# Graph layer with gathers, one-hot picks and sorted scatter: the broadcast of dst is issued one step earlier and first in SyncE's step

## The chip, the cores and the metric

The kernel runs on one core of one Trainium2 chip, written directly against the five engines (TensorE, VectorE, ScalarE, GpSimd, SyncE) with hand-placed semaphores. The metric is the device time of one execution in microseconds (us), median of three runs.

## The reference

```python
h = jnp.maximum(_layernorm(x, axis=-1), 0.0)                 # x: 100000 x 96
concat = jnp.concatenate([h[src], h[dst], edge_attr], axis=-1)   # 25000 edges, 96 + 96 + 64
gates = jax.nn.sigmoid(concat @ W_e + b_e)                   # 25000 x 96
messages = jax.nn.softplus(concat @ W_n + b_n)
gated = gates * messages
h_new = jax.ops.segment_sum(gated, dst, num_segments=n)
edge_count = jnp.clip(segment_sum(ones, dst), 1.0, None)[:, None]
x = x + h + h_new / edge_count
```

All edges are sorted by `dst`.

## The kernel before, in words

The 100000 nodes are cut into 49 chunks of 2048 rows (`CHUNK`, 16 tiles of 128 rows by 96), and the 25000 edges into 49 steps (`STEPS`) of 512 edges (`TB` = 4 tiles of 128). Every engine runs its own `step(i)` loop over the same index, each a few steps ahead of or behind the others, and semaphores tie them together.

What each engine does in one step:

- **SyncE (SP)** issues all plain transfers of the step from one queue: the edge attributes (`attr`), the load of node chunk i (`node_x`, 768 KB), the store of finished node chunk i - 4 (`out<-node_out`, 768 KB), and two broadcasts. `low_across` is two stretches of 400 values of the low bits of `dst`, each copied to all 128 partitions (2 x 200 KB). `dst_across` is the 512 `dst` values of one edge step, copied to all partitions (256 KB). The only thing that paces SP is the wait for `node_sum_done`, ahead of the node load: the buffer of chunk i - 4 must be read out.
- **VectorE (DVE)** finishes the layer norm factors of a chunk, normalizes 3 of its 16 tiles, then does for edge step m = s - 3 (s is its own step): `same` (line 732, which compares `dst_across` with the `dst` column, and waits for that broadcast), `same_prev`, `messages` (the product of gate and softplus). Then 13 statistics of the next node chunk (line 703), `onehot` (line 762, from `low_across`, and waits for it), the sum `node_out` (line 801), which raises `node_sum_done`, then the edge statistics, the counts and `final` of edge step m, and the variance.
- **TensorE (PE)** picks the normalized rows of the destinations with the one-hot matrix (`picks`, line 950, 2 x 8 tiles), transposes the source rows and attributes, sums the messages of equal `dst` (`sums`, lines 962 and 963, which waits for `messages` and `same`), and computes the products `z` (lines 1016 to 1018).
- **ScalarE (ACT)** normalizes the other 13 tiles and does the exponentials and logarithms.
- **GpSimd (POOL)** gathers four tiles of source rows (line 396) and scatters four tiles of `final` with accumulation into `out` (line 417).

`dst_across` and `onehot` have two buffers each, `low_across` and `same` one, `node_x` and `node_out` four. Semaphore names used below: `same_done` counts two for each edge step that DVE has compared, `onehot_done` one for each one-hot matrix.

In step index: SP's step i is released by the node sum of DVE's step i - 5. DVE's step s compares edge step s - 3, and makes the one-hot matrix of chunk s + 2. The loop of DVE that uses what SP's step i brings:

```python
def equality(m):
    wait(dve, across_loaded[m % 2], m // 2 * 16 + 16)
    wait(dve, sum_done, m)
...
def one_hot(n):
    wait(dve, low_loaded, 32 * (n + 1))
    wait(dve, pick_done, 2 * (n - 1))
```

Of the kernel before, what the change touches and what calls it, by code (L numbers as in the profile page):

```python
# [10 lines left out]
P = 128  # L11
# [4 lines left out]
TB = 4  # L16
STEPS = TILES // TB
# [25 lines left out]
def build(nc, x, src, dst, edge_attr, w_e, b_e, w_n, b_n, out, count_table, dst_pad, low_pad):  # L43
    ctx = ExitStack()
    with ctx:
        def sb(name, shape, dt=FP32):
            return ctx.enter_context(nc.sbuf_tensor(name, shape, dt))
# [4 lines left out]
        def sem(name):  # L52
            return ctx.enter_context(nc.semaphore(name))

        def sems(name, n=NS):
            return [sem(f"{name}{u}") for u in range(n)]
# [58 lines left out]
        dst_across = [sb(f"dst_across{v}", [P, TB, P], I32) for v in range(2)]  # L115
# [61 lines left out]
        dst_stored = sem("dst_stored")  # L177
# [17 lines left out]
        across_loaded = sems("across_loaded", 2)  # L195
# [34 lines left out]
        same_done = sem("same_done")  # L230
# [37 lines left out]
        def runs_step(i):  # L268
            return 0 <= i < STEPS
# [10 lines left out]
        def wait(eng, semaphore, value):  # L280
            if value > 0:
                eng.wait_ge(semaphore, value)

        def chunk_dmas(n):

            return 16 * (n // NS + 1) + (16 if n == STEPS - 1 else 0)

        def move_chunk(eng, n, t, tile, inward, done):
            lo = n * CHUNK
            if n < STEPS - 1:  # L290
                parts = [(t[lo:lo + CHUNK, :].rearrange("(r p) d -> p r d", p=P), tile[:, :, :])]
            else:
                mid = lo + LAST_FULL * P
                parts = [(t[lo:mid, :].rearrange("(r p) d -> p r d", p=P), tile[:, 0:LAST_FULL, :]),
                         (t[mid:NODES, :], tile[0:LAST_PART, LAST_FULL, :])]
            for far, near in parts:
                eng.dma_start(near if inward else far, far if inward else near).then_inc(done, 16)  # L297

        def load_index_rows(eng, n, t, shift_by, loaded):
            half = P * P  # L300
            full = (TILES - 1) * P
            k = LAST_EDGES - shift_by
            eng.dma_start(index_rows[:, n, 0, :], t[shift_by:shift_by + half].rearrange("(t e) -> t e", e=P)).then_inc(loaded, 16)
            eng.wait_ge(padding_done, 1)
            eng.dma_start(index_rows[0:TILES - 1 - P, n, 1, :],
                          t[half + shift_by:full + shift_by].rearrange("(t e) -> t e", e=P)).then_inc(loaded, 16)
            eng.dma_start(index_rows[TILES - 1 - P:TILES - P, n, 1, 0:k],
                          t[full + shift_by:EDGES].rearrange("(a e) -> a e", a=1)).then_inc(loaded, 16)

        dst_flat = dst_pad.rearrange("t e -> (t e)")  # L310
        low_flat = low_pad.rearrange("t e -> (t e)")

        def first_at(eng, cell):
            return eng.value_load(cell, min_val=0, max_val=TILES * P)  # L314

        @block.sync
        def _(sp):
            load_index_rows(sp, 0, dst, 0, dst_rows_loaded)

            def load_low(n):  # L320
                first, second = (first_at(sp, first_row[0:1, 2 * n + h:2 * n + h + 1]) for h in range(2))
                wait(sp, onehot_done, n)
                for h, at in ((0, first), (1, second)):
                    sp.dma_start(low_across[:, h, :],  # L324
                                 low_flat[bass.ds(at, SPAN)].partition_broadcast(P)).then_inc(low_loaded, 16)

            def step(i):
                n = i - LEAD
                tail = (STEPS - 1) * TB * P
                if runs_step(n):  # L330
                    wait(sp, attr_trans_done, n - NS + 1)
                    if n == STEPS - 1:
                        m = (TB - 1) * P
                        sp.dma_start(attr[n % NS][:, 0:TB - 1, :],
                                     edge_attr[tail:tail + m, :].rearrange("(t p) f -> p t f", p=P)).then_inc(attr_loaded[n % NS], 16)
                        sp.dma_start(attr[n % NS][0:LAST_EDGES, TB - 1, :],
                                     edge_attr[tail + m:EDGES, :]).then_inc(attr_loaded[n % NS], 16)
                    else:
                        ev = edge_attr[0:tail, :].rearrange("(b t p) f -> b p t f", t=TB, p=P)
                        sp.dma_start(attr[n % NS][:, :, :], ev[n, :, :, :]).then_inc(attr_loaded[n % NS], 16)  # L340
                j = i - NS
                if runs_step(j):
                    wait(sp, node_sum_done, j + 1)
                if runs_step(i):
                    move_chunk(sp, i, x, node_x[i % NS], True, node_loaded[i % NS])
                if runs_step(j):
                    move_chunk(sp, j, out, node_out[j % NS], False, node_stored[j % NS])
                if i == 0:
                    load_index_rows(sp, 2, dst, 1, next_rows_loaded)
                if i == NS - 1:  # L350
                    sp.wait_ge(place_done, 2)
                    sp.dma_start(first_row[0:1, :].rearrange("a (p b) -> a p b", b=1),
                                 place_i[0:HALVES, BLOCKS:BLOCKS + 1]).then_inc(place_loaded, 16)
                    sp.dma_start(place_row[0:1, :].rearrange("a (p b) -> a p b", b=BLOCKS),
                                 place_i[0:HALVES, 0:BLOCKS]).then_inc(place_loaded, 16)
                    sp.wait_ge(place_loaded, 32)
                    sp.wait_ge(low_stored, 16)
                    load_low(0)
                n = i - 2
                if i >= NS - 1 and runs_step(n):  # L360
                    load_low(n)

                k = i - 7
                if runs_step(k):
                    if k == 0:
                        sp.wait_ge(dst_stored, 16)
                    wait(sp, same_done, 2 * (k - 1))
                    sp.dma_start(dst_across[k % 2][:, :, :].rearrange("p t e -> p (t e)"),
                                 dst_flat[k * TB * P:(k + 1) * TB * P].partition_broadcast(P)).then_inc(across_loaded[k % 2], 16)

            for i in range(STEPS + 7):
                step(i)
            for u in range(NS):
                sp.wait_ge(node_stored[u], chunk_dmas(STEPS - 1 - (STEPS - 1 - u) % NS))
# [704 lines left out]
```

## Time and profile before

| | |
|---|---|
| median of three runs | 948.62 us (947.77 to 948.77) |
| profiled execution, its own time | 951.04 us |
| span of the profiled execution | 949.3 us |
| mean granted TensorE clock | 0.792 |
| TensorE matmul busy | 605.9 us, 64% of the span |
| VectorE busy | 546.1 us, 58% |
| ScalarE busy | 520.5 us, 55% |
| GpSimd busy | 512.4 us, 54% |
| data moved | 136.32 MB, mean 144 GB/s |

The busy times are those of the profiled execution; shares are of its span. The loop's steps look alike from about 100 us to 870 us, so that one step read in detail stands for all.

### The profile page before, as it was taken

How to read it: one execution, taken by the hardware profiler on the slowest of the kernel's cores; microseconds unless marked ns; L12 is line 12 of the kernel's file. 1: busy time of each engine (PE TensorE's matmuls, PEld its weight loads, DVE VectorE, ACT ScalarE, POOL GpSimd, SP SyncE). 2: the span in 40 equal slices, each digit the busy share in tenths (PEclk: the TensorE clock that was granted, in tenths of full speed). 3: DMA queues.
4: the chain of work that ended last, by engine and by line, in shares of the span. 5: the costliest groups of instructions: out<-in, count | busy, mean ns of one | idle time of the engine just before them, and what ended most of it. 6: DMA issues, size and time to landing. Idle time of an engine off the chain costs nothing.

```text
span 949.3 us, 15042 instructions
## 1 busy us (share of the span) xinstructions
PE 605.9 (64%) x3832; PEld 578.3 (61%) x3832; DVE 546.1 (58%) x2203; ACT 520.5 (55%) x1330; POOL 512.4 (54%) x404
## 2 busy tenths in 40 slices
PE   0255777667656765775776677567667657758971
PEld 0255777567556765764766566567667656747871
DVE  5667466466546645654664665466466456548551
ACT  0356655655564565466456546645655654665660
POOL 5211355654565466466556546655654664666676
PEclk9997778878777787778787778778778777878795
DMA  8277757766785677687577668767866865875652
GB/s 202 55 176 162 156 126 166 161 138 141 159 158 125 151 165 149 132 176 154 124 165 164 137 136 173 152 122 160 164 143 148 165 150 125 182 150 121 113 82 18
DMA packets 285403, 136.32 MB, mean 144 GB/s; under 512 B 262207, under 2 KB 275848, under 8 KB 285320
## 3 DMA queue, kind: packets, MB, share of 16 engines
q1 hardware_dynamic: 249214, 116.34, 52.8%
q0 software_dynamic: 34576, 18.40, 14.4%
q10 hardware_dynamic: 1530, 0.61, 0.3%
q8 instruction: 35, 0.57, 0.3%
q14 instruction: 48, 0.39, 0.1%
HBM read 88.16 MB, written 48.30 MB: 144 GB/s over the span
## 4 chain that ended last, share of the span: by engine, by line
DMA 33%; SPq 26%; DVE 26%; issue 8%; PE 3%; POOL 2%; DVEq 0%; ACT 0%; POOLq 0%; ACTq 0%
DMA dst_across<-dst_pad 30%; SPq L324 11%; SPq L297 10%; DVE stats L703 9%; DVE node_out L801 9%; SPq L314 6%; DVE messages L725 3%; DVE onehot L762 3%; POOL out L417 2%; DMA low_across<-low_pad 2%; PE pick_ps L950 1%; DVE same_prev L735 1%; DVE dst_t L645 1%; DMA dst_t<-dst_pad,first_tile_i 1%; DMA dst_t<-in_src 1%
## 5 line engine op out<-in xcount | busy, mean ns | idle before, releaser
L417 POOL DMA_INDIRECT out<-final,scatter_idx x196 | 309.7, 1580 | 317.9 <-DVE final L717 251.1
L962 PE MATMUL sums_ps<-messages,same 128*128 128x97 f32 x392 | 123.3, 415 | 247.5 <-DVE messages L725 247.5
L484 ACT ACTIVATE node_out<-node_x,shift,rstd 128x96 f32<-128x96 f32 x637 | 261.7, 458 | 12.5 <-DVE shift L756 12.5
L396 POOL DMA_INDIRECT edge_x<-in_x,src_idx x196 | 200.6, 1023 | 111.2 <-issue 58.8
L962 PEld LDWEIGHTS sums_ps<-messages,same 128*128 128x128 f32 x392 | 99.7, 312 | 254.1 <-DVE messages L725 254.0
L732 DVE TENSOR_TENSOR same<-dst_across,dst_col 128x512 f32<-128x512 int32 x49 | 34.0, 693 | 327.6 <-DMA dst_across<-dst_pad 327.6
L950 PE MATMUL pick_ps<-onehot,node_out 128*96 x1568 | 165.2, 263 | 61.0 <-ACT node_out L484 44.9
L950 PEld LDWEIGHTS pick_ps<-onehot,node_out 128*96 128x96 f32 x1568 | 156.6, 178 | 77.5 <-issue 77.2
L490 ACT ACTIVATE log_var<-var 128x20 f32<-128x20 f32 x52 | 11.4, 218 | 321.1 <-DVE var L827 321.1
L703 DVE BATCH_NORM_STATS2 stats<-node_x 128x6 f32<-128x96 f32 x784 | 142.2, 243 | 0.0
L963 PE MATMUL sums_ps<-messages,same_prev 128*128 128x97 f32 x392 | 118.4, 402 | 0.0
L1016 PE MATMUL z_ps<-w_src,src_t 97*128 97x192 f32 x392 | 117.8, 388 | 0.0
L1017 PE MATMUL z_ps<-w_dst,dst_t 96*128 96x192 f32 x392 | 109.5, 365 | 0.0
L1018 PE MATMUL z_ps<-w_attr,attr_t 128*128 128x192 f32 x392 | 104.9, 351 | 0.0
L963 PEld LDWEIGHTS sums_ps<-messages,same_prev 128*128 128x128 f32 x392 | 101.8, 318 | 0.0
L801 DVE TENSOR_TENSOR node_out<-node_out,node_x 128x1536 f32<-128x1536 f32 x49 | 85.8, 1750 | 5.9 <-PE pick_ps L950 5.9
L1017 PEld LDWEIGHTS z_ps<-w_dst,dst_t 96*128 96x128 f32 x392 | 83.5, 225 | 0.0
L1016 PEld LDWEIGHTS z_ps<-w_src,src_t 97*128 97x128 f32 x392 | 83.1, 236 | 0.0
L1018 PEld LDWEIGHTS z_ps<-w_attr,attr_t 128*128 128x128 f32 x392 | 79.1, 214 | 0.0
L514 ACT ACTIVATE src_h<-edge_x,shift,rstd 128x96 f32<-128x96 f32 x196 | 74.9, 452 | 1.8 <-DVE shift L756 1.8
L502 ACT ACTIVATE dst_t<-pick_ps 96x336 f32 x98 | 43.4, 443 | 52.0 <-PE pick_ps L950 44.7
L549 ACT ACTIVATE log1p<-log1p 128x768 f32<-128x768 f32 x49 | 41.3, 842 | 0.1
(107 smaller groups left out, 624.1 us busy)
## 6 DMA issues: line engine op xcount, KB each, us to landing
node_x<-in_x SPq DMA_DIRECT2D x48, 768.0 KB, 5.2
out<-node_out SPq DMA_DIRECT2D x48, 768.0 KB, 7.8
low_across<-low_pad SPq DMA_DIRECT2D x98, 200.0 KB, 6.0
dst_across<-dst_pad SPq DMA_DIRECT2D x49, 256.0 KB, 6.2
attr<-in_edge_attr SPq DMA_DIRECT2D x48, 128.0 KB, 6.4
edge_x<-in_x,src_idx POOLq DMA_INDIRECT x196, 2.8
out<-final,scatter_idx POOLq DMA_INDIRECT x196, 6.1
node_x<-in_x SPq DMA_DIRECT2D x1, 624.0 KB
```

The lines of the kernel that those rows point to most:

```text
L324: sp.dma_start(low_across[:, h, :], low_flat[bass.ds(at, SPAN)].partition_broadcast(P)).then_inc(low_loaded, 16)
L396: nc.gpsimd.indirect_dma_start(out=edge_x[i % NS][:, t, :], out_offset=None, in_=x, in_offset=bass.IndirectOffsetOnAxis(ap=src_idx[:, i * ...
L417: nc.gpsimd.indirect_dma_start(out=out, in_=final[j % FINALS][:, t, :], in_offset=None, out_offset=bass.IndirectOffsetOnAxis(ap=scatter_id ...
L484: last = nc.scalar.activation(node_out[n % NS][:, r, :], node_x[n % NS][:, r, :], ACT.Relu, bias=shift[us][:, c:c + 1], scale=rstd[us][:, ...
L703: last = nc.vector.bn_stats(stats[:, TB + r, :], node_x[c % NS][:, r, :])
L801: nc.vector.tensor_tensor(node_out[d % NS][:, :, :], node_out[d % NS][:, :, :], node_x[d % NS][:, :, :], ALU.add).then_inc(node_sum_done, 1)
L950: last = nc.tensor.matmul(pick_ps[0:D, bass.ds(a, WINDOW)], node_out[d % NS][:, h * BLOCKS + b, :], onehot[d % 2][:, h, bass.ds(a, WINDOW) ...
L962: nc.tensor.matmul(sum_ps[:, t, :], same[:, t, :], cur, start=True, stop=False)
L963: last = nc.tensor.matmul(sum_ps[:, t, :], same_prev[:, t, :], prev, start=False, stop=True)
L1016: nc.tensor.matmul(z, src_t[0:D + 1, t, :], w_src[0:D + 1, :], start=True, stop=False)
L1017: nc.tensor.matmul(z, dst_t[0:D, e:e + P], w_dst[0:D, :], start=False, stop=False)
L1018: last = nc.tensor.matmul(z, attr_t[:, t // 2, :], w_attr[t % 2][:, :], start=False, stop=True)
```

## The change

SP's block for the broadcast of `dst` moves within the step, and its index changes from i - 7 to i - 6. It is issued after the wait for `node_sum_done` and ahead of the node load and store; the code of the broadcast itself is the same, and SP's loop is one step shorter. No other engine's code is touched.

```diff
                 if runs_step(j):
                     wait(sp, node_sum_done, j + 1)
+                k = i - 6
+                if runs_step(k):
+                    if k == 0:
+                        sp.wait_ge(dst_stored, 16)
+                    wait(sp, same_done, 2 * (k - 1))
+                    sp.dma_start(dst_across[k % 2][:, :, :].rearrange("p t e -> p (t e)"),
+                                 dst_flat[k * TB * P:(k + 1) * TB * P].partition_broadcast(P)).then_inc(across_loaded[k % 2], 16)
                 if runs_step(i):
                     move_chunk(sp, i, x, node_x[i % NS], True, node_loaded[i % NS])
                 if runs_step(j):
...
                 if i >= NS - 1 and runs_step(n):
                     load_low(n)

-                k = i - 7
-                if runs_step(k):
-                    if k == 0:
-                        sp.wait_ge(dst_stored, 16)
-                    wait(sp, same_done, 2 * (k - 1))
-                    sp.dma_start(dst_across[k % 2][:, :, :].rearrange("p t e -> p (t e)"),
-                                 dst_flat[k * TB * P:(k + 1) * TB * P].partition_broadcast(P)).then_inc(across_loaded[k % 2], 16)
-
-            for i in range(STEPS + 7):
+            for i in range(STEPS + 6):
                 step(i)
```

On SP, in the middle of the program, one step of the kernel before reads so (the attributes first, the broadcast of `dst` last):

```order
L340 DMA attr<-in_edge_attr 128x4x64 [waits attr_trans_done]
L297 DMA node_x<-in_x 128x16x96 [waits node_sum_done]
L297 DMA out<-node_out 128x16x96
L314 TENSOR_LOAD dst_t
L314 ISA x2
L324 REGISTER_ALU [waits onehot_done]
L324 DMA low_across<-low_pad 128x400
L324 REGISTER_ALU
L368 DMA dst_across<-dst_pad 128x512 [waits same_done]
```

The same step of the changed kernel:

```order
L340 DMA attr<-in_edge_attr 128x4x64 [waits attr_trans_done]
L349 DMA dst_across<-dst_pad 128x512 [waits same_done,node_sum_done]
L297 DMA node_x<-in_x 128x16x96
L297 DMA out<-node_out 128x16x96
L314 TENSOR_LOAD dst_t
L314 ISA x2
L324 REGISTER_ALU [waits onehot_done]
L324 DMA low_across<-low_pad 128x400
L324 REGISTER_ALU
```

(In both, the pair of register loads and the low broadcast stand twice; one of each is left out.) The broadcast has moved from behind both low broadcasts to the head of what the node sum releases, and it now carries both waits.

On DVE, which waits for both broadcasts, nothing moves. One step of it reads in both kernels, from the end of the normalization on:

```order
L787 TENSOR_SCALAR node_out<-node_out 128x288 [waits dve_part_done]
L732 TENSOR_TENSOR same<-dst_across,dst_col 128x512 [waits sum_done,across_loaded0]
L735 TENSOR_TENSOR same_prev<-dst_across,dst_col 32x4x32 [waits ones_done]
L725 TENSOR_TENSOR messages<-log1p 128x4x96 [waits sum_done,ones_done,softplus_done,gate_done]
L703 BN_STATS stats<-node_x 128x6 x13
L762 TENSOR_SCALAR onehot<-low_across,lane 128x800 [waits pick_done,low_loaded]
L801 TENSOR_TENSOR node_out<-node_out,node_x 128x1536 [waits pick_done,dve_norm_done,node_norm_done]
```

What moved is which of SP's steps fills the buffer that `same` reads: before, SP's step that is released by the node sum of the step just ahead of this one; after, the one before that.

## Rows read from the trace of the kernel before

**Rows 1.** The page: busy share of two engines, and the chain by engine.

```profile
PE 605.9 (64%) x3832; PEld 578.3 (61%) x3832; DVE 546.1 (58%) x2203; ACT 520.5 (55%) x1330; POOL 512.4 (54%) x404
...
DMA 33%; SPq 26%; DVE 26%; issue 8%; PE 3%; POOL 2%; DVEq 0%; ACT 0%; POOLq 0%; ACTq 0%
```

**Rows 2.** The waits of all engines: total us, times, longest.

```profile
DVE same L732 <- DMA dst_across<-dst_pad: 327.6, 46, 9.4
...
DVE onehot L762 <- DMA low_across<-low_pad: 17.0, 4, 5.2
```

**Rows 3.** The waits of SP's own queue.

```profile
SPq L297 <- DVE node_out L801: 533.0, 49, 12.9
```

**Rows 4.** Timeline of one step: start, busy us, engine, line, what, idle before.

```profile
399.14 1.75 DVE L801 TENSOR_TENSOR node_out<-node_out,node_x 128x1536 f32<-128x1536 f32 x1
...
400.92 0.38 SPq L297 DMA_DIRECT2D node_x<-in_x  x1
...
401.35 1.67 SPq L297 DMA_DIRECT2D out<-node_out  x1
...
403.60 1.62 POOL L417 DMA_INDIRECT out<-final,scatter_idx  x1 [5.83 <-DVE final L717]
...
404.67 2.22 SPq L324 DMA_DIRECT2D low_across<-low_pad  x2
...
405.50 0.36 DVE L787 TENSOR_SCALAR node_out<-node_out 128x288 f32<-128x288 f32 x1
...
406.93 0.43 SPq L368 DMA_DIRECT2D dst_across<-dst_pad  x1
...
407.40 1.57 PE L950 MATMUL pick_ps<-onehot,node_out 128*96 x16
...
413.58 0.69 DVE L732 TENSOR_TENSOR same<-dst_across,dst_col 128x512 f32<-128x512 int32 x1 [7.72 <-DMA dst_across<-dst_pad]
...
415.10 2.17 DVE L703 BATCH_NORM_STATS2 stats<-node_x 128x6 f32<-128x96 f32 x13
...
415.40 0.94 POOL L396 DMA_INDIRECT edge_x<-in_x,src_idx  x1 [0.30 <-issue]
...
417.18 0.62 DVE L762 TENSOR_SCALAR onehot<-low_across,lane 128x800 f32<-128x800 f32 x1
...
417.72 1.75 DVE L801 TENSOR_TENSOR node_out<-node_out,node_x 128x1536 f32<-128x1536 f32 x1
```

**Rows 5.** The chain that ended last, same step: issue of the second low broadcast.

```profile
406.53 0.35 SPq L324
```

**Rows 6.** Transfers issued between 400 and 418.6 us: size, median us to landing.

```profile
low_across<-low_pad SPq DMA_DIRECT2D x2, 200.0 KB, 6.4
dst_across<-dst_pad SPq DMA_DIRECT2D x1, 256.0 KB, 6.6
```

**Rows 7.** Timeline of DVE in an early step, ahead of the first dst broadcast.

```profile
59.41 1.75 DVE L801 TENSOR_TENSOR node_out<-node_out,node_x 128x1536 f32<-128x1536 f32 x1
...
71.86 0.64 DVE L762 TENSOR_SCALAR onehot<-low_across,lane 128x800 f32<-128x800 f32 x1 [3.56 <-DMA low_across<-low_pad]
```

**Rows 8.** Timeline of DVE: first and last node sum around 43 steps with a dst broadcast.

```profile
87.37 1.76 DVE L801 TENSOR_TENSOR node_out<-node_out,node_x 128x1536 f32<-128x1536 f32 x1 [1.72 <-PE pick_ps L950]
...
872.19 1.75 DVE L801 TENSOR_TENSOR node_out<-node_out,node_x 128x1536 f32<-128x1536 f32 x1
```

**Rows 9.** Timeline of POOL at the end of the program.

```profile
902.67 1.55 POOL L417 DMA_INDIRECT out<-final,scatter_idx  x1 [4.28 <-DVE final L717]
...
912.84 1.55 POOL L417 DMA_INDIRECT out<-final,scatter_idx  x1 [3.02 <-DVE final L717]
```

**Rows 10.** Windows: busy us of each engine, then PEclk, DMA share, GB/s.

```profile
411.70:413.60 1.90, 0.00 (x0) 0.00 (x0) 0.02 (x1) 1.90 (x5) 1.44 (x2) 0.50 1.10 241
...
100.00:870.00 770.00, 517.76 (x3296) 494.64 (x3295) 449.52 (x1812) 444.80 (x1143) 433.57 (x333) 0.78 0.70 150
```

## The prediction

> **What bounds the kernel now.** I read the page first: no engine is near full, TensorE is the busiest with 64% [rows 1], and the chain that ended last runs for a third through transfers and for a quarter each through SP's issuing and DVE. So it is a loop of latencies, not of work. The waits name the transfer: DVE waited 46 times for the broadcast of dst, 327.6 us in all, or 7.1 us a step; for the low broadcast only four times [rows 2]. SP in turn waited all 49 times for the node sum, 533.0 us [rows 3]. These two waits close the loop.
>
> The timeline of one step shows it whole [rows 4]. The node sum ends at 399.14 + 1.75 = 400.89 us. SP issues the node load at 400.92, the store at 401.35, the low broadcasts from 404.67, the second of them at 406.53 [rows 5], and at 406.93 the dst broadcast. DVE has been ready for it since 405.50 + 0.36 = 405.86, and starts `same` at 413.58, so the broadcast is taken to land there, 12.69 us behind the node sum. Then come `same`, messages and 13 statistics, `onehot` at 417.18, and the next node sum at 417.72. The step took 18.58 us; 43 such steps took 872.19 - 87.37 = 784.82 us, 18.25 each [rows 8].
>
> **What the change does to a step.** The broadcast that `same` needs was issued in the same DVE step that waits for it. Now it is issued one node sum earlier, so it has a whole step more and the 7.1 us wait goes. Its buffer is free: SP's step i now waits until edge step i - 8 has been compared, and DVE does that in its step i - 5 ahead of the very node sum that releases SP. So `same_done` should never be the later of the two waits, and costs nothing; if it were late, the node load, the store and both low broadcasts would stand behind it.
>
> The stall does not go whole, because `onehot` waits for the low broadcasts of the same SP step, which is released by the node sum just ahead. Today that wait is covered by the dst wait and the work behind it. What is late next is therefore the second low broadcast. DVE would have its statistics done 417.18 - 413.58 = 3.60 us after it starts `same` at 405.86, at about 409.5, and then stands until the low broadcast lands.
>
> When does it land? Today it was issued at 406.53, and the two of this window took 6.4 us in the median [rows 6]: 412.9. The moved issue costs SP 0.43 us ahead of it [rows 4], so by its issue it lands at 406.53 + 0.43 + 6.4 = 413.36. `onehot` then starts at 413.36 instead of 417.18: **3.82 us less a step**. I take this value. From below and above:
>
> - If the broadcast of dst holds up all that is behind it by its own transfer time, the last of the queue lands when the last of the queue landed before, at 413.58. The same bytes from the same release must be moved. Saving 3.60 us.
> - In the early step without a dst broadcast and with no scatter yet, `onehot` started at 71.86, 10.72 us behind the node sum's end at 59.41 + 1.75 [rows 7]. That was for 768 + 768 + 400 = 1936 KB; 256 KB more at this rate is 1.42 us, so 12.14 us, landing at 413.03. Saving 4.15 us. It leaves out the scatters, so I hold it for the optimistic end.
>
> The Trainium skill ("DMA: Bandwidth & Descriptors", section on queues, rings and completion order) says that each DMA engine consumes the descriptors of one ring in order. That speaks for the first of these, against my 3.82. By that rule the sum is some 9 us smaller; this trace agrees so far as the dst broadcast, issued last, lands 0.65 us behind the second low one. I stay between the two because the dst broadcast also no longer shares the engines with the end of the low ones.
>
> **Is there other cover for 3.8 us?** The step would be 18.25 - 3.82 = 14.43 us. POOL from its first scatter to its last gather needs 415.40 + 0.94 - 403.60 = 12.74 us [rows 4]; it fits with 1.7 us to spare. DVE's own work is 546.1 / 49 = 11.1 us, TensorE's 605.9 / 49 = 12.4 us [rows 1]. TensorE had its second picks done at 407.40 + 1.57 = 408.97, 8.1 us into the step, so they are not late for a node sum at 12 to 13 us. The node load has one full step between landing and use. The transfers: a DMA share of 0.70 over 18.25 us [rows 10] is 12.8 us a step, 0.89 of 14.43; tight, but one window shows 1.10 [rows 10], so 0.89 is no wall. It leaves little room for anything beyond the forecast.
>
> **The sum.** 43 steps by 3.82 us is 164 us. The steps ahead of 87.37 us gain nothing: there the low broadcast, or the picks, ended the wait [rows 7, 8], and in one of them the dst broadcast is now added, under the 1.72 us that DVE waited for the picks. Behind 872.19 the last dst waits also go, but POOL's scatters are what ends: it waited 4.28 and 3.02 us for `final` there [rows 9], 7.3 us that can close; I take 6 of it, with 0 and 9 as bounds. Together 170 us. The profiled execution took 951.04 us, so 781; the median of the runs is 2.4 us lower, so **779 us**.
>
> **Rivals.**
>
> - *The low broadcast lands where the dst broadcast did* (the rule above as a mechanism): 43 x 3.60 + 6 = 161 us, so 788. Chance 0.23; my forecast 0.44.
> - *It lands earlier*, 4.15 us a step: 178 + 6, so 765, down to about 750. For it: the dst broadcast moves into the queue's empty start. Against it: the scatters run just then. Chance 0.13.
> - *Contention or a slower chain gives part back.* The gathers end at 416.34 [rows 4], and the next node sum will end at about 415.6, so their last transfers meet the next step's; a TensorE that starts its picks at the low clock reads its rows later, and ACT behind it. Each us a step is 43 us. With 0.5 to 1.2 us lost: 800 to 830. Chance 0.17.
> - *Slower than before: TensorE falls to its low level and becomes the bound.* In the idle time ahead of 413.6 us its granted clock was already 0.50, which is 1.2 GHz [rows 10]. If the new rhythm kept it there throughout, its 517.76 us of busy time over 770 us at a mean of 0.78 would be 12.3 x 0.78 / 0.50 = 19.1 us a step, over today's 18.25: some 37 us slower, 985. It decides once the mean clock is under 0.78 x 12.3 / 18.25 = 0.52. Against it: the engine idles less, not more, since `messages` come 7 us sooner. Chance 0.02.
> - *The change does not do what it says*: `same_done` is late after all and the node load waits for it, or `same` still waits, and the time stays at 949. By the order of DVE's step there is no room for it. Chance 0.01.
>
> **How the numbers follow.** The range goes from 755 to 812: it takes in the forecast, the in-order rival, most of the earlier landing, and losses up to 0.75 us a step, together about 0.83. About 0.2% (2 us) is what a measurement of this kernel can tell from no change. Faster takes all but the last two cases, 0.97; same 0.01, slower 0.02.
>
> **What the next profile would show.** DVE's wait for the dst broadcast near zero in the middle of the program, and in its place a wait of `onehot` for the low broadcast in nearly every step, 3.5 to 4 us each, some 160 us in all. Node sums 14.2 to 14.8 us apart. Issue to landing of the low broadcast still 6 to 6.7 us; 7.5 or more would be contention. SP waiting for the node sum about 3.8 us less a step, and not for `same_prev`. POOL's wait for `final` down from about 5.8 to about 2 us. A mean TensorE clock above 0.78. I am wrong if `onehot` does not wait (then another engine sets the step), if the picks end the wait of the node sum, or if the low broadcast takes much longer once gathers and scatters of neighbouring steps meet in the DMA engines.

## The result, and the profile after

The changed kernel takes 834.48 us (832.53 to 835.17, four runs) beside 948.26 us for the kernel before: ratio 0.8797, 95% interval 0.8781 to 0.8813. That is 114 us less, where 170 were forecast, and outside the forecast range, whose upper end was 812. The wait that was to go has gone, and the one that was to be late next is late, but for longer than forecast.

The page of the profile after, the lines that answer to [rows 1]:

```profile
span 833.4 us, 15088 instructions
...
PE 583.6 (70%) x3832; PEld 564.9 (68%) x3832; DVE 546.9 (66%) x2203; ACT 524.5 (63%) x1330; POOL 521.6 (63%) x404
...
SPq 39%; DMA 34%; DVE 12%; issue 9%; POOL 3%; PE 1%; ACT 0%; POOLq 0%; ACTq 0%; DVEq 0%
```

The transfers' share of the chain is as before, DVE's has halved (the work between the dst broadcast and `onehot` is no longer on it), and SP's issuing has grown from 26% to 39%. That last number is the first sign of what the forecast missed.

The waits of all engines (total, times, longest), beside [rows 2]:

```profile
DVE onehot L761 <- DMA low_across<-low_pad: 227.8, 48, 5.8
...
POOL out L416 <- DVE final L716: 133.9, 38, 21.5
```

and SP's own, beside [rows 3]:

```profile
SPq L349 <- DVE node_out L800: 333.9, 47, 7.9
...
SPq L349 <- DVE same_prev L734: 9.8, 2, 6.7
```

The dst broadcast stands in no line of DVE's waits any more; the low broadcast does, 4.7 us a time. In its new place the wait for `same_done` cost SP 9.8 us in the whole program, in two waits (`same_prev` is the second comparison, which raises it).

One step of the changed kernel, in the order of its timeline (start, busy us, engine and line, idle before), beside [rows 4]. SP issues the broadcast of dst, the node load, the store, then the two low broadcasts:

```profile
402.40 1.75 DVE L800 TENSOR_TENSOR node_out<-node_out,node_x 128x1536 f32<-128x1536 f32 x1
...
404.18 0.33 SPq L349 DMA_DIRECT2D dst_across<-dst_pad  x1
...
404.55 0.43 SPq L297 DMA_DIRECT2D node_x<-in_x  x1
...
405.03 3.69 SPq L297 DMA_DIRECT2D out<-node_out  x1
...
409.05 0.68 DVE L731 TENSOR_TENSOR same<-dst_across,dst_col 128x512 f32<-128x512 int32 x1
...
410.59 1.65 SPq L324 DMA_DIRECT2D low_across<-low_pad  x2
...
418.26 0.64 DVE L761 TENSOR_SCALAR onehot<-low_across,lane 128x800 f32<-128x800 f32 x1 [5.54 <-DMA low_across<-low_pad]
...
418.81 1.75 DVE L800 TENSOR_TENSOR node_out<-node_out,node_x 128x1536 f32<-128x1536 f32 x1
```

The node load is issued 2.15 us behind the node sum's start, 0.4 us later than before, as forecast. But the issue of the store takes 3.69 us instead of 1.67, and the first low broadcast is issued 410.59 - 402.40 = 8.19 us behind the node sum's start; in [rows 4] it was 404.67 - 399.14 = 5.53. I read the long issue as SP standing before a queue that takes no more until it drains; the profile shows the time of the issue, not its reason. The issues by kind (SP's transfers, with size and median us from issue to landing), first the changed kernel:

```profile
node_x<-in_x SPq DMA_DIRECT2D x48, 768.0 KB, 7.0
...
low_across<-low_pad SPq DMA_DIRECT2D x98, 200.0 KB, 5.8
dst_across<-dst_pad SPq DMA_DIRECT2D x49, 256.0 KB, 4.1
```

and two of them in the kernel before:

```profile
node_x<-in_x SPq DMA_DIRECT2D x48, 768.0 KB, 5.2
low_across<-low_pad SPq DMA_DIRECT2D x98, 200.0 KB, 6.0
```

The node load lands 1.8 us later behind its issue than before, the low broadcasts 0.2 us sooner. The first and the last node sum around the same 43 steps as in [rows 8]:

```profile
87.66 1.75 DVE L800 TENSOR_TENSOR node_out<-node_out,node_x 128x1536 f32<-128x1536 f32 x1
...
761.46 1.75 DVE L800 TENSOR_TENSOR node_out<-node_out,node_x 128x1536 f32<-128x1536 f32 x1
```

That is 673.8 us, 15.67 a step instead of 18.25: 2.58 us saved, where 3.82 were forecast. The 1.24 us of difference by 43 steps are 53 us, nearly the whole of the miss of 55 us (the span fell by 115.9 us: 111.0 in these steps, 5.2 behind them, less 0.3 lost ahead of them).

### The profile page after: what moved, and what is told of

Same layout as the page of the kernel before. It is cut to its first block, busy times and chain, and to the rows that moved or that the text cites. A ratio compares the mean times of both kernels' runs of the same rounds, so it can differ in the third digit from the quotient of the medians.

```text
span 833.4 us, 15088 instructions
## 1 busy us (share of the span) xinstructions
PE 583.6 (70%) x3832; PEld 564.9 (68%) x3832; DVE 546.9 (66%) x2203; ACT 524.5 (63%) x1330; POOL 521.6 (63%) x404
## 4 chain that ended last, share of the span: by engine, by line
SPq 39%; DMA 34%; DVE 12%; issue 9%; POOL 3%; PE 1%; ACT 0%; POOLq 0%; ACTq 0%; DVEq 0%
DMA low_across<-low_pad 33%; SPq L297 21%; DVE node_out L800 10%; SPq L324 8%; SPq L314 8%; POOL out L416 3%; SPq L349 2%; PE pick_ps L949 1%; DVE dst_t L644 1%; DMA dst_t<-dst_pad,first_tile_i 1%; DMA dst_t<-in_src 1%; DVE onehot L761 0%; POOL edge_x L395 0%; ACT node_out L483 0%; DMA dst_t<-place_i 0%
## 5 line engine op out<-in xcount | busy, mean ns | idle before, releaser
L949 PE MATMUL pick_ps<-onehot,node_out 128*96 x1568 | 230.1, 327 | 212.5 <-ACT node_out L483 204.6
L949 PEld LDWEIGHTS pick_ps<-onehot,node_out 128*96 128x96 f32 x1568 | 223.6, 241 | 226.9 <-issue 226.9
L761 DVE TENSOR_SCALAR onehot<-low_across,lane 128x800 f32<-128x800 f32 x49 | 32.1, 654 | 227.8 <-DMA low_across<-low_pad 227.8
L1015 PE MATMUL z_ps<-w_src,src_t 97*128 97x192 f32 x392 | 99.5, 335 | 0.0
L961 PE MATMUL sums_ps<-messages,same 128*128 128x97 f32 x392 | 85.0, 302 | 3.7 <-DVE messages L724 3.7
L962 PE MATMUL sums_ps<-messages,same_prev 128*128 128x97 f32 x392 | 83.6, 298 | 0.0
L961 PEld LDWEIGHTS sums_ps<-messages,same 128*128 128x128 f32 x392 | 67.2, 215 | 4.0 <-DVE messages L724 3.9
L1015 PEld LDWEIGHTS z_ps<-w_src,src_t 97*128 97x128 f32 x392 | 69.0, 196 | 0.0
L962 PEld LDWEIGHTS sums_ps<-messages,same_prev 128*128 128x128 f32 x392 | 67.3, 215 | 0.0
L995 PE MATMUL trans_ps<-ident,src_h 128*96 128x128 f32 x196 | 49.1, 402 | 3.0 <-ACT src_h L513 3.0
```

What stands on the lines that cost most here:

```text
L949: last = nc.tensor.matmul(pick_ps[0:D, bass.ds(a, WINDOW)], node_out[d % NS][:, h * BLOCKS + b, :], onehot[d % 2][:, h, bass.ds(a, WINDOW) ...
L961: nc.tensor.matmul(sum_ps[:, t, :], same[:, t, :], cur, start=True, stop=False)
L962: last = nc.tensor.matmul(sum_ps[:, t, :], same_prev[:, t, :], prev, start=False, stop=True)
L1015: nc.tensor.matmul(z, src_t[0:D + 1, t, :], w_src[0:D + 1, :], start=True, stop=False)
```

## The experiments

Two theories stood at the start of the experiments. **A**: the place costs, because the broadcast at the head of the queue holds everything behind it back by about 2 us. **B**: the shorter step costs, because transfers of neighbouring steps now meet. All ratios are to the kernel before on the same chip; "us a step" is the mean of the same 43 steps throughout.

**The lead without the place** (e1_lead_only). Against the kernel before, only the index changes: the broadcast is issued one step sooner, but still last, behind the low broadcasts.

```diff
                     load_low(n)

-                k = i - 7
+                k = i - 6
                 if runs_step(k):
...
-            for i in range(STEPS + 7):
+            for i in range(STEPS + 6):
```

> The broadcast of dst one step sooner, but left at the end of SP's step, behind the low broadcasts. Theory A (its place at the head costs: it held the node load and store back by about 2 us, so that the low broadcasts were issued at 7.98 us instead of 5.47 us behind the start of the node sum): the low broadcast is issued at about 5.5 us again, onehot starts about 14.0 us behind the node sum's start, the step takes 14.4 to 14.8 us, the time is 775 to 795 us. Theory B (the shorter step makes the transfers of neighbouring steps meet, wherever the broadcast stands): the step stays near 15.8 us and the time near 834 us.

790.53 us, ratio 0.8348 (0.8327 to 0.8369). Its timeline:

```profile
399.25 1.75 DVE L801 TENSOR_TENSOR node_out<-node_out,node_x 128x1536 f32<-128x1536 f32 x1
...
405.23 1.89 SPq L324 DMA_DIRECT2D low_across<-low_pad  x2
...
412.93 0.64 DVE L762 TENSOR_SCALAR onehot<-low_across,lane 128x800 f32<-128x800 f32 x1 [3.31 <-DMA low_across<-low_pad]
413.48 1.75 DVE L801 TENSOR_TENSOR node_out<-node_out,node_x 128x1536 f32<-128x1536 f32 x1
```

The low broadcast is issued 5.98 us behind the node sum's start (5.68 in the mean of 35 steps), `onehot` waits 3.3 us, and the 43 steps take 14.56 us each. So a step of 14.6 us is possible and B falls: the place at the head cost some 43 us (0.8797 against 0.8348 of the kernel before).

**The place without the lead** (e2_place_only). Against the changed kernel:

```diff
-                k = i - 6
+                k = i - 7
...
-            for i in range(STEPS + 6):
+            for i in range(STEPS + 7):
```

> The broadcast of dst first in what the node sum releases, but for the same edge step as before (index i - 7), so no step sooner. In the changed kernel it lands 4.1 us behind its issue, and VectorE comes to the comparison 4.9 us behind the end of the node sum, so theory A says that the place alone does all of what the change did: 830 to 840 us. A theory in which the lead of one step is what removed the wait says that a wait on dst returns and the time is above 860 us.

835.67 us, ratio 0.8829 (0.8807 to 0.8852), the step 15.64 us. DVE's longest wait in total is again the low broadcast:

```profile
DVE onehot L761 <- DMA low_across<-low_pad: 202.2, 44, 6.4
```

So the place alone does what the whole change did. Either part removes the wait for dst; both together gain nothing that is clear of noise over the place alone, and the lead alone gains some 43 us more.

**The same bytes without a common source** (e3_plain_source). Its 128 rows of 2 KB are loaded from 128 places in x (`plain_rows` is x cut into rows of 512 values).

```diff
-                                 dst_flat[k * TB * P:(k + 1) * TB * P].partition_broadcast(P)).then_inc(across_loaded[k % 2], 16)
+                                 plain_rows[k * P:(k + 1) * P, :]).then_inc(across_loaded[k % 2], 16)
```

> The changed kernel, with the broadcast of dst replaced by a load of the same size and shape (128 rows of 2 KB) whose rows lie one behind the other in x, so the comparison works on other numbers and the output is not the reference's. Theory A1 (a broadcast is slow because all 16 DMA engines read the same 2 KB): its 128 packets take about 1 us instead of 2.6 us, the low broadcasts are issued 1 to 1.5 us sooner, and the time falls to 775 to 800 us. Theory A2 (any 256 KB at the head costs as much): 828 to 838 us. Theory B: also 828 to 838 us.

796.02 us, ratio 0.8408 (0.8393 to 0.8423), 14.67 us a step. It is in the same place and moves the same 256 KB, and costs 0.11 us a step over the lead without the place, where the broadcast costs 1.11. What the queue moves behind the node sum shows the difference. First the changed kernel, three windows of 1 us that begin 1 us behind the end of a node sum (length, busy us of PE, PEld, DVE, ACT and POOL with their instructions, then TensorE clock, DMA share, GB/s):

```profile
357.48:358.48 1.00, 0.00 (x0) 0.00 (x0) 1.00 (x6) 0.12 (x1) 0.00 (x0) 1.00 0.32 123
358.48:359.48 1.00, 0.00 (x0) 0.00 (x0) 1.00 (x4) 1.00 (x5) 0.30 (x1) 1.00 0.72 158
359.48:360.48 1.00, 0.22 (x3) 0.23 (x3) 0.96 (x8) 1.00 (x4) 1.00 (x1) 1.00 0.81 171
```

The same windows of e3_plain_source:

```profile
343.19:344.19 1.00, 0.00 (x0) 0.00 (x0) 1.00 (x7) 0.07 (x1) 0.00 (x0) 1.00 0.91 143
344.19:345.19 1.00, 0.00 (x0) 0.00 (x0) 1.00 (x4) 1.00 (x5) 0.26 (x1) 1.00 1.08 330
345.19:346.19 1.00, 0.17 (x2) 0.18 (x3) 0.96 (x8) 1.00 (x3) 1.00 (x1) 1.00 1.24 294
```

With the broadcast at the head the 16 DMA engines move 123, 158 and 171 GB/s in the first three busy microseconds; with the plain rows 143, 330 and 294. The trace also records each packet; a row of a transfer is one packet here. In the mean of some 35 steps, and leaving out the first and the last 2% of a transfer's packets, the 128 packets of the dst broadcast take 2.27 us, those of the plain load 1.26 us. The packets of node load and store begin 4.5 us behind the node sum's start instead of 4.3 (3.1 before) and end at 10.6 instead of 9.7 (8.7 before). The broadcast does not run alone: while it runs, 267 packets of node load and store start beside its own, against 21 beside the plain rows in their shorter time.

**Ahead of the low broadcasts instead of ahead of the load** (e5_ahead_of_low). Against the kernel before:

```diff
-                n = i - 2
-                if i >= NS - 1 and runs_step(n):
-                    load_low(n)
-
-                k = i - 7
+                k = i - 6
                 if runs_step(k):
...
+                n = i - 2
+                if i >= NS - 1 and runs_step(n):
+                    load_low(n)
```

> The broadcast of dst one step sooner, issued behind the node load and store and just ahead of the low broadcasts. Theory A-ring (a slow broadcast holds up whatever stands behind it in SP's queue, wherever it stands): the low broadcasts land about as late as in the changed kernel, the step is 15.4 to 15.9 us, 820 to 840 us. Theory A-head (it is the head that costs, because the large load cannot start): the step is 14.5 to 14.9 us, 785 to 800 us.

829.58 us, ratio 0.8732 (0.8703 to 0.8760), 15.44 us a step. SP's timeline:

```profile
400.88 0.39 SPq L297 DMA_DIRECT2D node_x<-in_x  x1
...
403.07 3.50 SPq L364 DMA_DIRECT2D dst_across<-dst_pad  x1
...
407.87 0.94 SPq L324 DMA_DIRECT2D low_across<-low_pad  x2
```

So it is not the head that costs: the load is issued at once here. In both places tried in front of the transfer that the loop waits for, the broadcast costs about the same. Its issue took 3.50 us, against 0.33 at the head, which I read in the same way as the store's.

**From another queue** (e6_act_queue). The block leaves SP and stands at the head of ScalarE's step, for the edge step that is compared one step later (SP's own block is deleted, which is not shown).

```diff
+                if runs_step(j):
+                    if j == 0:
+                        act.wait_ge(dst_stored, 16)
+                    wait(act, same_done, 2 * (j - 1))
+                    act.dma_start(dst_across[j % 2][:, :, :].rearrange("p t e -> p (t e)"),
+                                  dst_flat[j * TB * P:(j + 1) * TB * P].partition_broadcast(P)).then_inc(across_loaded[j % 2], 16)
```

> The broadcast of dst issued from ScalarE's queue, at the head of its step, one step sooner than it is used; SP's queue holds only attributes, load, store and low broadcasts. Theory A-ring: SP's low broadcasts are issued 5.5 to 5.7 us behind the node sum's start again and the step is 14.3 to 14.8 us, 780 to 800 us. A theory in which the broadcast's slow packets hold the DMA engines themselves, whatever queue they come from: 14.9 to 15.7 us a step, 805 to 835 us.

773.14 us, ratio 0.8115 (0.8094 to 0.8137), 14.18 us a step, faster than the first of the two expectations. The low broadcast is issued at 5.67 us again. ScalarE issues the broadcast 3.9 us behind the node sum's start, so its packets run in the middle of node load and store. It costs nothing there that can be seen, and its 128 packets took only 1.27 us. Three windows of one step, in which the broadcast's packets ran from 406.5 to 408.3:

```profile
406.30:407.30 1.00, 1.00 (x8) 1.00 (x8) 0.89 (x4) 1.00 (x5) 0.69 (x2) 0.50 1.25 280
407.30:408.30 1.00, 1.00 (x8) 1.00 (x8) 0.94 (x3) 0.44 (x2) 1.00 (x1) 0.50 1.04 309
408.30:409.30 1.00, 1.00 (x8) 0.97 (x8) 1.00 (x5) 0.32 (x1) 0.70 (x2) 0.50 1.20 310
```

So 128 rows from one source need not be slow: this is the rate of the plain rows, and it is the same source as in the changed kernel. The step is some 0.4 us shorter than with the broadcast behind the low ones in SP's queue; why by that much was not settled.

**Half the bytes, as many packets** (e7_half_bytes): 128 rows of 1 KB, against the changed kernel.

```diff
-                    sp.dma_start(dst_across[k % 2][:, :, :].rearrange("p t e -> p (t e)"),
-                                 dst_flat[k * TB * P:(k + 1) * TB * P].partition_broadcast(P)).then_inc(across_loaded[k % 2], 16)
+                    tiles = TB if k < 2 else TB // 2
+                    sp.dma_start(dst_across[k % 2][:, 0:tiles, :].rearrange("p t e -> p (t e)"),
+                                 dst_flat[k * TB * P:(k * TB + tiles) * P].partition_broadcast(P)).then_inc(across_loaded[k % 2], 16)
```

> The changed kernel, with only the first two of four tiles of dst broadcast from the third edge step on (128 KB, rows of 1 KB instead of 2 KB); the comparison of the other two tiles works on old numbers, so the output is not the reference's. Theory A (time in the queue grows with the broadcast's bytes from one source): about half of the 1.1 us a step that the place costs comes back, the low broadcasts are issued at about 7.0 instead of 8.0 us, the step is 14.9 to 15.2 us, 800 to 815 us. If the cost is one per packet (there are still 128), the step stays at 15.6 us and the time at 830 us or more.

831.88 us, ratio 0.8746 (0.8716 to 0.8775), 15.49 us a step. The expectation from bytes fell; the other one written beside it holds. The windows behind a node sum:

```profile
358.99:359.99 1.00, 0.00 (x0) 0.00 (x0) 1.00 (x7) 0.08 (x1) 0.00 (x0) 1.00 0.53 78
359.99:360.99 1.00, 0.00 (x0) 0.00 (x0) 1.00 (x4) 1.00 (x5) 0.27 (x1) 0.66 1.01 128
360.99:361.99 1.00, 0.18 (x1) 0.19 (x2) 0.96 (x8) 1.00 (x4) 1.00 (x1) 0.50 0.91 215
```

In the first two windows the rate is 78 and 128 GB/s, against 123 and 158 with all bytes: with half the bytes the broadcast fills nearly the same time.

**Half the packets** (e8_half_rows): 64 rows of 2 KB, against the changed kernel.

```diff
-                    sp.dma_start(dst_across[k % 2][:, :, :].rearrange("p t e -> p (t e)"),
-                                 dst_flat[k * TB * P:(k + 1) * TB * P].partition_broadcast(P)).then_inc(across_loaded[k % 2], 16)
+                    rows = P if k < 2 else P // 2
+                    sp.dma_start(dst_across[k % 2][0:rows, :, :].rearrange("p t e -> p (t e)"),
+                                 dst_flat[k * TB * P:(k + 1) * TB * P].partition_broadcast(rows)).then_inc(across_loaded[k % 2], 16)
```

> The changed kernel, with dst broadcast to 64 of the 128 partitions from the third edge step on (64 rows of 2 KB, 128 KB); the other half compares old numbers, so the output is not the reference's. With half the bytes in 128 rows nothing came back (the broadcast's packets took 2.0 us instead of 2.3 us, the step 15.49 us). Theory per-packet (one source is read at one packet per about 16 ns, whatever its length): 64 packets take about 1.1 us, about 1 us of the step comes back, 14.5 to 14.9 us a step, 785 to 805 us. Theory of a fixed cost of one broadcast at the head: 2 us stay, 15.4 us a step, 825 us or more.

809.20 us, ratio 0.8490 (0.8451 to 0.8529), 14.96 us a step: 0.71 us of the 1.11 that the place costs came back. The time lies between the two expectations, 4 us above the end of the first and 16 below the second, so a fixed cost falls and a cost by packets holds only roughly. Its windows:

```profile
347.85:348.85 1.00, 1.00 (x8) 1.00 (x7) 1.00 (x6) 0.11 (x1) 0.00 (x0) 1.00 0.51 89
348.85:349.85 1.00, 0.34 (x3) 0.05 (x1) 1.00 (x4) 1.00 (x5) 0.29 (x1) 1.00 0.78 192
349.85:350.85 1.00, 0.21 (x2) 0.21 (x3) 0.96 (x8) 1.00 (x4) 1.00 (x1) 1.00 1.13 297
```

The third window is at 297 GB/s, against 171 in the changed kernel. By the packet records the three kernels took 2.27 us for 128 packets of 2 KB (17.7 ns a packet), 2.03 us for 128 of 1 KB (15.9 ns) and 0.88 us for 64 of 2 KB (13.8 ns). The low broadcasts, 256 packets of 1.6 KB in 3.79 us, are 14.8 ns a packet. So at the head of SP's queue the broadcast's time goes mainly by its packets and hardly by its bytes.

That is no price for any place, though. The same 128 packets of 2 KB from the same source took 1.27 us from ScalarE's queue (9.9 ns a packet), and last in SP's queue 1.7 us in the kernel before and 2.4 us in e1_lead_only. What slows the broadcast in SP's queue is therefore not shown by these runs; e3_plain_source shows that it does not happen there with distinct rows of another tensor, e6_act_queue that the common source alone does not do it.

**The low broadcasts first** (e4_low_first), the version that the theory points to, and two relatives. Against the kernel before, with the broadcast of dst left last:

```diff
+                n = i - 2
+                if i >= NS and runs_step(n):
+                    load_low(n)
                 j = i - NS
                 if runs_step(j):
                     wait(sp, node_sum_done, j + 1)
...
-                if i >= NS - 1 and runs_step(n):
+                if i == NS - 1 and runs_step(n):
                     load_low(n)

-                k = i - 7
+                k = i - 6
```

> From the second full step on, the low broadcasts are issued ahead of the wait for the node sum, then the node load and store, then the broadcast of dst one step sooner, last. Theory A: no broadcast that VectorE waits for stands behind the load and store any more, the 228 us of waiting for the low broadcast shrink to under 60 us, and the step is set by a chain through the other engines, 13.0 to 14.5 us, 720 to 790 us. Theory B (the transfers of the step do not fit into less than 15.8 us): the wait moves to the node load or another transfer and the time stays above 820 us.

732.97 us, ratio 0.7748 (0.7732 to 0.7764), 13.32 us a step. No broadcast is left among the long waits:

```profile
ACT dst_t L505 <- PE pick_ps L953: 69.9, 36, 4.5
DVE node_out L804 <- PE pick_ps L953: 69.1, 38, 4.9
...
PE pick_ps L953 <- issue: 46.3, 35, 4.4
```

The chain that ended last now runs through TensorE and ScalarE:

```profile
PE 41%; ACT 30%; issue 11%; another core or an unknown queue 5%; DVE 3%; POOL 3%; SPq 2%; ACTq 2%; DMA 1%; POOLq 0%; DVEq 0%
```

The step is no longer set by SP's queue but by these two, the picks on TensorE above all (16% of the chain), which ScalarE and DVE wait for.

**The same with the broadcast of dst in ScalarE's queue** (e9_low_first_act). Its edit is that of e4_low_first for the low broadcasts and that of e6_act_queue for dst.

> Low broadcasts ahead of the wait for the node sum, as in the fastest kernel so far (ratio 0.775), and the broadcast of dst from ScalarE's queue. If the kernel with the low broadcasts first is still held by its queue, this is faster, ratio 0.75 to 0.77; if it is held by the chain through the picks on TensorE, it is the same within 1%, or slower by ScalarE's issue time (0.3 us a step, 0.79).

741.22 us, ratio 0.7781 (0.7749 to 0.7812), 13.46 us a step: the queue no longer matters, as the second expectation says.

**The same with the broadcast of dst at the head** (e10_low_first_dst_head). This is the changed kernel with only the low broadcasts moved ahead of the wait for the node sum.

> The changed kernel with only the low broadcasts moved ahead of the wait for the node sum, so the broadcast of dst still stands at the head of what the node sum releases. If the place costs only through the low broadcasts behind it, it costs nothing here: within 1% of the kernel with the low broadcasts first and dst last, ratio 0.77 to 0.785. If it costs through the node load and store too, ratio 0.80 or more.

735.68 us, ratio 0.7718 (0.7678 to 0.7757), 13.32 us a step, the same as with dst last. So the place costs only through the low broadcasts behind it; the later node load costs nothing, as the forecast had it ("one full step between landing and use").

## Why the prediction was wrong

- *The wait for dst goes, whole*: right. 327.6 us have become none, and e2 shows that the one step of lead was not even needed for it: the broadcast lands 4.1 us behind its issue and DVE asks for it 4.9 us behind the node sum's end.
- *`same_done` costs nothing*: right, 9.8 us in two places.
- *What is late next is the second low broadcast, since DVE stands for it with its statistics done*: right, 48 waits.
- *"The moved issue costs SP 0.43 us ahead of it [rows 4], so by its issue it lands at 413.36"*: **this is the step that failed.** It is the term of the sum that was mis-sized, and the bound behind it too. The second low broadcast, which this term is about, was issued 9.45 us behind the node sum's start in the mean, against 7.47 before: 2.0 us later, not 0.43 (the first one 7.98 against 5.47). Part came back, since it then landed 5.8 us behind its issue and not 6.4, and `onehot` started 15.25 us behind the node sum's start where the forecast put it at about 13.9 (its step of 14.43 less the 0.54 from `onehot` to the next node sum). I took SP's issue times as fixed. They are not: behind the slow broadcast the store's issue alone grew by 2 us.
- *One step taken for all*: a smaller part of the miss. In the mean of some 30 steps `onehot` started 17.89 us behind the node sum's start, where the step of [rows 4] had 18.04. With the mean values the same sum gives 17.89 - (7.47 + 0.43 + 6.4) = 3.59 us a step instead of 3.82.
- *The in-order rival* (788 us) had the right mechanism, that what is in front in the queue holds back what is behind, but too small a price. It lets the last of the queue land when the last landed before, 413.58 - 399.14 = 14.44 us behind the node sum's start, as if the queue did the same work in the same time in any order. But `onehot` started at 15.25: the broadcast's packets took 1.7 us at the end of the queue and 2.27 us at its head, where the 16 engines moved little more than half of their rate (158 and 171 GB/s in the second and third of the microseconds shown, against 330 and 294 with the plain rows). The bound of 4.15 us was too hopeful for the same reason: it priced the broadcast's 256 KB at the mean rate, 1.42 us. The Trainium skill ("DMA: Bandwidth & Descriptors", section on queues, rings and completion order) states that descriptors of one ring are consumed in order. The runs agree: behind the low broadcasts (e1) the step is 14.56 us, ahead of them (e5) 15.44, in another queue (e6) 14.18. Staying between the two bounds instead of following this cost 9 us of the 55; even the in-order price was 46 us short.
- *Contention between neighbouring steps* (800 to 830): the time came out just above its upper end, but not by its mechanism. With the lead alone the steps are closer still, and they take 14.56 us.
- *The 3.82 us a step*: the lead alone saves 18.25 - 14.56 = 3.69, close to it, but that is luck. With the 0.43 us for the place taken out, the same sum gives 4.25 for that edit.
- *"SP waiting for the node sum about 3.8 us less a step"*: it came out (533.0 / 49 = 10.9 us before, 333.9 / 47 = 7.1 after), but by luck again. The step is only 2.6 us shorter; the rest of SP's wait went into longer issues.
- *The tail*: 6 us forecast, 5.2 measured. *The slower rivals*: the mean granted clock rose from 0.792 to 0.823; TensorE did not stay at its low level.

What stays open is why the broadcast is slow in SP's queue and not in ScalarE's. That it is slow there, and holds back the low broadcasts, is shown; e3 changed the rows' addresses and their tensor together, and no run moved the broadcast in time within one queue without changing what runs beside it.

## What to carry to other kernels

When the transfer that a loop waits for is issued last, look not only at when the moved one is issued, but at what it will hold up: in one queue, a slow transfer in front delays all behind it, and the issuing engine too. Do not price a broadcast by its bytes at the mean rate: its packets took 14 to 18 ns each at the head of SP's queue, and 10 ns from ScalarE's. Put it behind what the loop waits for, or in another queue. And ask which transfer closes the loop after the edit: here moving the low broadcasts ahead of the node sum's wait, which they never needed, was worth another 99 us on top of the change (834.5 to 735.7 us, e10_low_first_dst_head).

## What was not expected of the hardware

- At the head of SP's queue, 128 rows from one 2 KB source took hardly longer than 128 rows from one 1 KB source (2.27 and 2.03 us), and nearly twice as long as 128 rows from 128 places (1.26 us).
- The time of an issue on SP depends on what was issued ahead of it: the store's went from 1.67 to 3.69 us with nothing changed in it, and that of the dst broadcast from 0.33 us at the head to 3.50 us behind load and store.
- The same broadcast from ScalarE's queue, beside a load in SP's, took 1.27 us for its 128 packets and did not hold the low broadcasts up.
